# DLRM tower with a two-layer CIN: tails of two groups in one masked operand, P's tiles 0 and 1 split, P ahead of A on TensorE, 128-row spreads

## The reference, cut to what matters

```python
e = stack([tbl_f[ids[:, f]] for f in range(32)], axis=1)      # 512 x 32 x 64
z  = einsum('bhd,bfd->bhfd', e, e)                            # layer 1: 32 x 32 products
y  = relu(einsum('bcd,oc->bod', z.reshape(B, 1024, D), w0) + b0)
hidden, direct1 = y[:, :64], y[:, 64:]
z  = einsum('bhd,bfd->bhfd', hidden, e)                       # layer 2: 64 x 32 products
direct2 = relu(einsum('bcd,oc->bod', z.reshape(B, 2048, D), w1) + b1)
z  = concatenate([direct1, direct2], axis=1).sum(-1)          # 512 x 192
h  = relu(concatenate([z, dense_ctx], 1) @ W_top1 + b_top1)
h  = relu(h @ W_top2 + b_top2);   return h @ W_top3
```

## Time and profile before

| what | value |
|---|---|
| runs | 1076.74, 1075.27, 1078.74 us (median 1076.74) |
| the profiled execution | 1077.73 us, of which the span is 1075.9 us |
| mean granted TensorE clock | 0.995 of full |
| TensorE busy | 1028.1 us (96%) |
| VectorE busy | 932.3 us (87%) |
| GpSimd busy | 916.9 us (85%) |
| ScalarE busy | 724.9 us (67%) |
| DMA | 183.87 MB, 171 GB/s on average |

### The profile page before, as it was taken

One profiled execution on the slowest core, in us unless ns is written; L12 is line 12 of the kernel. 1 busy time (PEld: TensorE's weight loads), 2 busy tenths in 40 slices (PEclk: granted clock), 3 DMA queues, 4 the chain that ended last, 5 costly groups with the idle time before them and its releaser, 6 DMA issues.

```text
span 1075.9 us, 10627 instructions
## 1 busy us (share of the span) xinstructions
PE 1028.1 (96%) x3447; PEld 649.9 (60%) x3447; DVE 932.3 (87%) x609; ACT 724.9 (67%) x794; POOL 916.9 (85%) x299
## 2 busy tenths in 40 slices
PE   2199999999999999999999999999999999999999
PEld 1035566666666666666666666666666666666664
DVE  2069999999998999999999899999989888988881
ACT  5036666677777677777776677677777777777761
POOL 6507877989999999999999999999998988898880
PEclk9989999999999999999999999999999999999999
DMA  6467877878788778777887787788776777677730
GB/s 170 103 148 189 192 184 179 192 188 189 177 191 191 171 183 191 185 188 173 195 188 172 170 193 179 175 195 190 181 172 162 177 176 171 162 177 181 159 76 0
DMA packets 140633, 183.87 MB, mean 171 GB/s; under 512 B 55633, under 2 KB 56273, under 8 KB 140450
## 3 DMA queue, kind: packets, MB, share of 16 engines
q1 hardware_dynamic: 135970, 178.93, 70.5%
q0 software_dynamic: 4096, 4.20, 2.2%
q10 hardware_dynamic: 512, 0.07, 0.0%
HBM read 174.66 MB, written 8.39 MB: 170 GB/s over the span
## 4 chain that ended last, share of the span: by engine, by line
PE 75%; DVE 8%; DMA 6%; issue 4%; SPq 4%; POOL 3%; ACT 1%; ACTq 0%; DVEq 0%
PE py L633 34%; PE py L649 12%; PE py L639 12%; PE py L640 12%; DVE zf L544 5%; DMA xs<-x_dram 5%; POOL emb L333 3%; SPq L274 1%; SPq L268 1%; SPq L285 1%; PE py L654 1%; DVE zl L564 1%; DVE pzS L553 1%; DVE zS L557 0%; PE py L668 0%
## 5 line engine op out<-in xcount | busy, mean ns | idle before, releaser
L343 POOL TENSOR_TENSOR zl<-zf,zh 128x2048 fp32r<-128x2048 f32 x167 | 767.7, 4610 | 98.8 <-ACT zh L416 96.8
L544 DVE TENSOR_TENSOR zf<-xs,hid 128x2048 f32<-128x2048 f32 x256 | 583.0, 2283 | 53.3 <-ACT hid L431 49.4
L633 PE MATMUL py<-zf,wf 128*128 128x512 f32 x1080 | 488.3, 595 | 1.9 <-DVE zf L544 1.9
L416 ACT ACTIVATE zh<-zf 128x2048 fp32r<-128x2048 f32 x185 | 353.5, 1911 | 98.9 <-DVE zf L544 95.7
L633 PEld LDWEIGHTS py<-zf,wf 128*128 128x128 f32 x1080 | 205.0, 190 | 212.7 <-issue 197.4
L639 PE MATMUL py<-zh,wh 128*128 128x512 f32 x740 | 290.1, 392 | 1.3 <-ACT zh L416 1.3
L640 PE MATMUL py<-zh,wl 128*128 128x512 f32 x740 | 289.8, 392 | 0.0
L649 PE MATMUL py<-zl,wh 128*128 128x512 f32 x740 | 228.0, 430 | 0.0
L649 PEld LDWEIGHTS py<-zl,wh 128*128 128x128 f32 x740 | 139.4, 188 | 69.4 <-issue 46.4
L333 POOL DMA_INDIRECT emb<-in_tbl,idx x128 | 149.0, 1164 | 30.5 <-issue 25.5
L639 PEld LDWEIGHTS py<-zh,wh 128*128 128x128 f32 x740 | 139.0, 188 | 34.6 <-ACT zh L416 3.0
(11 more groups left out here) (77 smaller groups left out, 338.5 us busy)
## 6 DMA issues: line engine op xcount, KB each, us to landing
xs<-x_dram SPq DMA_DIRECT2D x512, 256.0 KB, 5.3
xs<-x_dram SPq DMA_DIRECT2D x504, 64.0 KB, 2.1
x_dram<-emb SPq DMA_DIRECT2D x68, 64.0 KB, 5.6
emb<-in_tbl,idx POOLq DMA_INDIRECT x128, 4.7
x_dram<-emb SPq DMA_DIRECT2D x20, 96.0 KB, 5.4
x_dram<-emb SPq DMA_DIRECT2D x4, 384.0 KB
xs<-in_L_rec_w SPq DMA_DIRECT2D x2, 512.0 KB, 4.6
xs<-in_L_rec_w SPq DMA_DIRECT2D x1, 1024.0 KB, 7.3
```

The lines of the kernel that those rows point to most:

```text
L343: pool.tensor_tensor(zl[:, q], zf[:, s], zh[:, q].bitcast(F32), ALU.subtract).then_inc(lo["P"], 1)
L416: act.activation(zh[:, q], zf[:, s], ACT.Copy).then_inc(hi, 1)
L544: dve.tensor_tensor(zf[:, slot(u)], left, right, ALU.mult).then_inc(mult, 1)
L633: mm = pe.matmul(y, wf[:, w, h], zf[:, s, h], start=first and h == 0, stop=ends and h == T - 1)
```

## The change

**Tails of two groups.** Groups 2q-1 and 2q form pair q (group 0 is its own; PAIRS = 33). The operands of the tail product are two SBUF tensors `x0_pair` and `xt_pair`, of which rows 0 to 63 are the odd group's and rows 64 to 127 the even one's; each is loaded by four DMAs, one of the two tensors in each period. One VectorE product per pair makes `pzS`, ScalarE copies its high part to `zS_high`, and one scalar_tensor_tensor computes `zS` = `pzS` x `low_rows` - `zS_high`, where `low_rows` is 0 or 1 per block of 32 rows. The weights `wS` carry the signs. The tail matmul of a group takes 64 rows of `zS` and `wS`.

**Direct sums of two groups.** ScalarE writes the direct channels of two neighbouring groups into the two halves of `dir1` in SBUF, and VectorE sums both in one instruction into `sums1`. ScalarE places the sums into `zd` after every 16 groups (eight small copies in all).

**P's tiles 0 and 1 split.** A new mode H holds for P(g), g >= 2, if C(g-1) is not in mode V: 46 units. Tiles 2 and 3 stay fp32 (four passes), tiles 0 and 1 are split: ScalarE makes `zhP`, VectorE makes `zlP` after C's product, and TensorE does six fp32r passes. The last of them raises `y1_ready`. C of group 0 goes from mode V to mode P.

**Order on TensorE.** From period 1 on: main P(g+1) (tiles 2 and 3, or all), late B(g-1), the high half of P, tail(g+1), main A(g), the low half of P, late A(g), and then as before.

**The start.** `x32` and `spreads` have 128 rows; the rows from 32 on are set to zero by VectorE. The batches of the first gathers are 12, 12, 5 and 3 tables (before 12, 12, 6 and 2), and the load of field 31 into `x32` is issued by SP.

```diff
+    if name == "P" and g >= 2 and mode(("C", g - 1)) != "V":
+        return "H"
     if name in "PD" or unit == ("A", 0):
         return "F"
...
-        return "P" if g % 2 else "V"
+        return "P" if g % 2 or g == 0 else "V"
...
-FIRST_BATCHES = [(0, 0, 12), (0, 12, 12), (0, 24, 6), (0, 30, 2)]
+FIRST_BATCHES = [(0, 0, 12), (0, 12, 12), (0, 24, 5), (0, 29, 3)]
...
+def pair_groups(q):
+    if q == 0:
+        return 0, 0
+    return 2 * q - 1, min(2 * q, LAST)
+
+def pair_of(g):
+    return (g + 1) // 2, 0 if g % 2 or g == 0 else 1
...
-        x32 = sb("x32", [F, N])
+        x32 = sb("x32", [P, N])
...
-        spreads = sb("spreads", [F, T + 2, P])
+        spreads = sb("spreads", [P, T + 2, P])
...
# SP
+                if n == 3:
+                    sp.wait_ge(x32_cleared, 2)
+                    load_x32(sp, 31, x32_last)
...
-            def load_xt(k):
-                if k >= 2:
-                    sp.wait_ge(s_mult, k)
+            def load_pair(q, buf, r):
+                k = pair_groups(q)
+                if k[1] % GC == 0:
+                    sp.wait_ge(x_stored[k[1] // GC], 16 * STORES[k[1] // GC])
+                sp.wait_ge(s_mult, q)
                 for j in range(4):
-                    sp.dma_start(xt[F * j:F * j + F], run_of_rows(k, 16)).then_inc(xt_in, 16)
+                    sp.dma_start(buf[F * j:F * j + F, :], run_of_rows(k[j // 2], r)).then_inc(pair_in, 16)
...
                 if g + 2 < G:
-                    load_xt(g + 2)
+                    load_pair(g // 2 + 2, xt_pair if g % 2 else x0_pair, 16 if g % 2 else 0)
...
# ScalarE
             def copy_x0(k):
                 act.wait_ge(x0_in, 64 * k)
-                act.wait_ge(s_mult, k)
+                if k >= 2:
+                    act.wait_ge(mult, NTH["P", k - 1])
...
+                if mode(u) == "H":
+                    act.wait_ge(mult, NTH[u])
+                    if NTH_HALF[u] > 1:
+                        act.wait_ge(y1_ready, HALVES[NTH_HALF[u] - 2][1] + 1)
+                    act.activation(zhP[:], zf[:, slot(u), 0:2], ACT.Copy).then_inc(hi_half, 1)
...
-            def high_s(k):
-                act.wait_ge(s_mult, k + 1)
-                if k >= 1:
-                    act.wait_ge(y1_ready, k)
-                act.activation(zS[:], pzS[:], ACT.Copy).then_inc(s_hi, 1)
+            def high_s(q):
+                act.wait_ge(s_mult, q + 1)
+                if q >= 1:
+                    act.wait_ge(s_lo, q)
+                act.activation(zS_high[:], pzS[:], ACT.Copy).then_inc(s_hi, 1)
...
             def finish_dir1(k):
-                act.activation(py1[H:P, k % 2], py1[H:P, k % 2], ACT.Relu, bias=bias0[H:P]).then_inc(dir1_ready, 1)
+                if k >= 2:
+                    act.wait_ge(sum1_done, k // 2)
+                half = slice(H * (k % 2), H * (k % 2) + H)
+                act.activation(dir1[half, :], py1[H:P, k % 2], ACT.Relu, bias=bias0[H:P]).then_inc(dir1_ready, 1)
...
# VectorE
-                left, right = (xt, px0[:]) if k >= 1 else (xt_first, x0_first[:])
+                left, right = (xt_pair[:], x0_pair[:]) if q >= 1 else (xt_first, x0_first[:])
                 dve.tensor_tensor(pzS[:], left, right, ALU.mult).then_inc(s_mult, 1)
 
-            def low_s(k):
-                dve.wait_ge(s_hi, k + 1)
-                dve.tensor_tensor(zS[H:P], pzS[H:P], zS[H:P].bitcast(F32), ALU.subtract).then_inc(s_lo, 1)
+            def low_s(q):
+                dve.wait_ge(s_hi, q + 1)
+                if q >= 1:
+                    dve.wait_ge(y1_ready, 2 * q - 1)
+                dve.scalar_tensor_tensor(zS[:], pzS[:], low_rows[:], zS_high[:].bitcast(F32), ALU.mult, ALU.subtract).then_inc(s_lo, 1)
 
             def low(u):
+                if mode(u) == "H":
+                    dve.wait_ge(hi_half, NTH_HALF[u])
+                    dve.tensor_tensor(zlP[:], zf[:, slot(u), 0:2], zhP[:].bitcast(F32), ALU.subtract).then_inc(lo_half, 1)
...
-            def sum_1(k):
-                dve.wait_ge(dir1_ready, k + 1)
-                dve.tensor_reduce(zd[H:P, NS * k:NS * k + NS], py1[H:P, k % 2].rearrange("p (b d) -> p b d", d=D),
+            def sum_1(j):
+                dve.wait_ge(dir1_ready, 2 * j + 2)
+                dve.tensor_reduce(sums1[:, NS * j:NS * j + NS], dir1[:].rearrange("p (b d) -> p b d", d=D),
                                   AX_X, ALU.add).then_inc(sum1_done, 1)
...
                 products(("A", g))
-                sum_1(g)
+                if g % 2:
+                    sum_1(g // 2)
                 if g + 1 < G:
                     products(("P", g + 1))
-                    products_s(g + 1)
+                    if g % 2 == 0:
+                        products_s(g // 2 + 1)
                 products(("C", g))
                 if g + 1 < G:
-                    low_s(g + 1)
+                    low(("P", g + 1))
+                    if g % 2 == 0:
+                        low_s(g // 2 + 1)
...
# TensorE
+            def main_half(u):
+                if mode(u) == "H":
+                    pe.wait_ge(hi_half, NTH_HALF[u])
+                    for h in range(2):
+                        pe.matmul(bank(u), whP[:, h], zhP[:, h], start=False, stop=False)
+                        pe.matmul(bank(u), wlP[:, h], zhP[:, h], start=False, stop=False)
+
+            def late_half(u):
+                if mode(u) == "H":
+                    pe.wait_ge(lo_half, NTH_HALF[u])
+                    pe.matmul(bank(u), whP[:, 0], zlP[:, 0], start=False, stop=False)
+                    mm = pe.matmul(bank(u), whP[:, 1], zlP[:, 1], start=False, stop=True)
+                    mm.then_inc(y1_ready, 1)
+
             def tail(k):
-                pe.wait_ge(s_lo, k + 1)
-                pe.matmul(py1[:, k % 2], wS[:], zS[:], start=False, stop=True).then_inc(y1_ready, 1)
+                q, half = pair_of(k)
+                rows = slice(H * half, H * half + H)
+                pe.wait_ge(s_lo, q + 1)
+                ends = mode(("P", k)) == "F"
+                mm = pe.matmul(py1[:, k % 2], wS[rows, :], zS[rows, :], start=False, stop=ends)
+                if ends:
+                    mm.then_inc(y1_ready, 1)
...
             for g in range(G):
-                main(("A", g))
+                if g == 0:
+                    main(("A", g))
+                if g + 1 < G:
+                    main(("P", g + 1))
                 if g >= 1:
                     late(("B", g - 1))
                 if g + 1 < G:
-                    main(("P", g + 1))
+                    main_half(("P", g + 1))
                     tail(g + 1)
+                if g >= 1:
+                    main(("A", g))
+                if g + 1 < G:
+                    late_half(("P", g + 1))
                 late(("A", g))
```

More of the change, by code:

```diff
@@ L78 @@
 UNITS = [u for g in range(-1, G) for u in period(g)]
-WHOLE = [u for u in UNITS if mode(u) == "F"]
-SPLIT = [u for u in UNITS if mode(u) != "F"]
+WHOLE = [u for u in UNITS if mode(u) in "FH"]
+SPLIT = [u for u in UNITS if mode(u) in "PV"]
+HALVES = [u for u in UNITS if mode(u) == "H"]
 LOW = {m: [u for u in SPLIT if mode(u) == m] for m in "PV"}
@@ L84 @@
 NTH_SPLIT = {u: i + 1 for i, u in enumerate(SPLIT)}
+NTH_HALF = {u: i + 1 for i, u in enumerate(HALVES)}
 NTH_LOW = {u: i + 1 for m in "PV" for i, u in enumerate(LOW[m])}
@@ L131, in dlrm_tower @@
         bias1 = sb("bias1", [P, 1])
-        xs = sb("xs", [P, 3 * T + 2, N])
+        xs = sb("xs", [P, 3 * T + 1, N])
+        x0_pair = sb("x0_pair", [P, N])
+        xt_pair = sb("xt_pair", [P, N])
         zf = sb("zf", [P, ZF, T, N])
@@ L212, in need_used @@
         def need_used(eng, u):
-            if mode(u) == "F":
+            if mode(u) in "FH":
                 eng.wait_ge(used_whole, NTH_WHOLE[u])
@@ L216, in need_used, with load_x32 @@
                 eng.wait_ge(used_split, NTH_SPLIT[u])
+        def load_x32(eng, f, landed):
+            eng.dma_start(x32[f:f + 1, :], emb[0:NS, 0, f, :]).then_inc(landed, 16)
         block = ctx.enter_context(nc.Block())
@@ L300, in _ @@
             load_xd(1)
-            load_xt(1)
+            load_pair(1, x0_pair, 0)
+            load_pair(1, xt_pair, 16)
             load_xe(0)
@@ L364, in _ @@
             act.wait_ge(turns_ready, 1)
+            act.wait_ge(x32_cleared, 2)
             for n, (first, step) in enumerate([(0, 0)] + [(4 * t, 1) for t in range(T)] + [(16, 0)]):
-                act.activation(spreads[:, n].rearrange("p (j i) -> p j i", i=F), view(turns, first, [[step, 4], [1, F]], F),
+                act.activation(spreads[0:F, n].rearrange("p (j i) -> p j i", i=F), view(turns, first, [[step, 4], [1, F]], F),
                                ACT.Copy).then_inc(turns_ready, 1)
@@ L446, in finish_2 @@
                 act.activation(py2[:, g % 2], py2[:, g % 2], ACT.Relu, bias=bias1[:]).then_inc(dir2_ready, 1)
-            for n in range(len(FIRST_BATCHES)):
-                load_x32(n)
+            for n in range(2):
+                _, f, m = FIRST_BATCHES[n]
```

(20 more changed lines are left out.)

101 lines of the change are left out of this document (65 added, 36 removed).

## The result

| | before | changed |
|---|---|---|
| median of 6 runs each, us | 1076.12 (1074.8 to 1080.0) | 1193.45 (1191.34 to 1195.54) |
| span of the profiled execution, us | 1075.9 | 1191.3 |
| end of tail 0 on TensorE | 66.7 | 59.6 |
| tail 1 to tail 11 | 158.7 | 161.0 |
| tail 11 to tail 43 | 492.2 | 590.9 |

The ratio is 1.1081, 95% interval 1.1057 to 1.1105: 117 us slower, where +49 was forecast. The table cuts each execution at the ends of tail matmuls. 99 us of the loss lie in the 32 middle periods.

The account below looks back on a forecast made before the run. TensorE was taken to bound the kernel, without gaps, at about 15.36 us a period. Start -6, early +2, middle +33 and late +20 sum to +49 on 1077.73: 1126 us, own range 1096 to 1150, full range 1077 to 1154.

Parts of the forecast that it names:

- TensorE's own terms: TensorE's passes: split P -0.34 us per unit (-15.6 in all), 64-row tails +0.4 each (+26 in all).
- The 64-row tail: Tail matmul among 128-row ones: each change of row count costs 0.2 us, two per tail, 26 us over 64 tails.
- The start: Earlier spreads by about 1.3 us and a clock that stays full with 128 rows: together -6 us (bounds -1.3, -7).
- Early periods: Periods 1 to 10: TensorE needs 31.9 us a pair, +0.5 a pair, +2 us with the ramp.
- The exclusion: A VectorE operation with two SBUF operands and a GpSimd subtraction exclude each other for their whole length.
- Late periods: Periods 43 to 62: VectorE waits for GpSimd, +1.0 us a period, +20 us over 20 periods (10 to 31).
- The tie at low A: Late even periods, tail product level with GpSimd's low A: 16.6 us if VectorE is first, 18.7 if GpSimd is.
- The middle: Periods 11 to 42: 14 us of VectorE waits in six periods, +1.04 a period, +33 us over 32 (16 to 51).
- the tail product's wait: Periods 11 to 42, tail product held by GpSimd: waits of 2.0, 0.2 and 1.9 us in six periods.
- P ahead of A: TensorE's new order: asks for P's product about 2.7 us earlier, 2 us in hand, so it costs nothing.
- Tails only: Rival: the exclusion falls into gaps and TensorE stays the bound, +4.4 us, 1081 us; chance 0.07.
- The gain comes through: Rival: TensorE bounds and 64 rows cost nothing, -6 - 15.6, 1055 us; chance 0.14.

Follow-up runs that it names:

- e8: The kernel before, with the tail product reading x0 from an SBUF copy made by ScalarE in place of PSUM: 1279.54 us, ratio 1.187.
- e1: The changed kernel, with the tail product reading one operand from PSUM (ScalarE copies x0_pair there): 1127.95 us, ratio 1.047.
- e15: The changed kernel with its 4-byte tensor low_rows padded to 64 bytes, nothing else: 1195.26 us, ratio 1.108.
- e18: The changed kernel, padded to 64 bytes and with TensorE's order of before: 1168.50 us, ratio 1.085.
- e9: The changed kernel, not padded, with GpSimd's second gather moved from ahead of low B to behind it: 1158.50 us, ratio 1.075.
- e16: The changed kernel, padded, with TensorE's order of before and GpSimd's second gather moved behind low B: 1120.69 us, ratio 1.039.
- e12: e11 with TensorE's order of before in place of P ahead of A: 1064.50 us, ratio 0.987.
- e3: The changed kernel with the tail product reading one operand from PSUM and P whole in fp32: 1103.51 us, ratio 1.025.
- e11: e3 with 128-row tails and low_rows padded to 64 bytes: 1070.96 us, ratio 0.993.
- e14: e6 with one unused tensor of 4 bytes per partition ahead of the operands, no instruction changed: 1079.08 us, ratio 1.001.
- e6: The kernel before with the new start alone (128-row x32 and spreads, new first batches, one load on SP): 1070.87 us, ratio 0.994.

## Why the forecast had the sign and missed the size

**TensorE's own terms held.** The 64-row tail was put at 0.4 us and measured 0.39. The start was put at -6 and gave -7.1 (59.6 against 66.7), at full clock. Early periods were put at 31.9 a pair; they took 32.04, and 31.79 with the padding.

**The exclusion held.** The half lows and tail products end a fixed 1.08 and 0.57 us after a GpSimd subtraction. e8 shows the exclusion alone, e1 its removal from the tail products. The sum of its waits is another matter (the middle, below).

**Late periods held, the number by luck.** +18.5 was measured, +20 forecast. The forecast averaged two cases of a tie, +0.5 and +1.55 a period. The tie at low A fell to VectorE each time, the cheaper case, for which +0.5 is 10 us; with TensorE's 15.42 for the odd periods in place of 15.2 it would be 13. For that case 16.6 and 15.42 were given, and 16.87 and 15.55 came: +0.85 a period. The 0.13 of difference in the second is the placement (15.38 in e15); that in the first is not explained.

**The middle failed: +33 forecast, +98.7 measured.** VectorE's time between tails 11 and 43 can be added up from the traces. A wait is a duration less 0.69 (tail product) or 1.21 (half low); the forecast's column is its 4.1 and 9.75 us in six periods, over 32.

| us | forecast | changed | e18 order of before | e9 gather moved | e16 both |
|---|---|---|---|---|---|
| waits in tail products | 22 | 84.5 | 84.8 | 22.3 | 22.2 |
| waits in half lows | 52 | 18.5 | 21.3 | 34.6 | 38.1 |
| VectorE idle | 0 | 39.8 | 16.2 | 45.5 | 12.4 |
| the middle | 525 | 590.9 | 568.6 | 554.5 | 522.6 |

The rest, VectorE's own work, is 446 to 452 us in each column (the forecast's 84.4 in six periods are 450). So the tail products' waits and the idle time were put too low, by 62 and 40 us, and the half lows' waits too high, by 33, which hid a third of the miss. Two steps are at fault.

The first is the tail product's wait, put at 2.0, 0.2 and 1.9 us in six periods. It was measured at 5.7, 5.7 and 4.3. The bookkeeping ended each wait at the end of the subtraction then running, though it had GpSimd's low B run on into the next period with low A right behind it. A tail product that waits does not get in between these two (a half low does between low A and low C, as shown above). Held so long, VectorE comes to its half lows when low A is over: that is why these waited less than forecast, and why they wait more again once the gather is moved. What the earlier trace rows shows held the hint: GpSimd's 9.15 for two subtractions without a gap at 440.88, and line 564 at 449.50 waiting for the end of the last. It met only the second, so the row didn't decide. Price: 35 us (e9), 48 once the order is right (e18 to e16).

The second is "P ahead of A: 2 us in hand, so nothing". The step asked only whether P's product is there in time. It left out what is moved back: B's last passes of the group before, behind P's main ones. ScalarE's ReLU waits for them and VectorE's second sum for it: 14.0 us of idle VectorE in the window shown, at the time when VectorE bounds. With the order of before VectorE's idle time in the middle falls from 37.3 (e15) to 16.2 us (e18), and the middle from 588.4 to 568.6. Price: 27 us (e18), 38 with the gather moved (e9 to e16, which has the padding too), 6.5 in a kernel that TensorE bounds (e12).

With both taken out, e16 is the kernel that the forecast described: 1120.7 us against 1126, middle 522.6 against 525, early 158.7 against 161, late 322.9 against 327. So the remaining terms are right together, in part because two errors offset each other: the table has 14 us less in the half lows than forecast and 12 us of idle time that was not in the forecast. The range ended at 1154 because its upper ends varied the waits' length and never their number.

**The rivals.** Nearest to "Tails only" is e3, which has neither the waits nor the split: 1103.5, where the forecast's terms for it, -6 and +26, give 1096; the other 8 us are the placement. "The gain comes through" was never near: with all of e11's edits the time is 1071, and there P's split was tried in the early groups alone, where it gives 2 us. What the change gains is the start; what was free of cost besides it is 128-row tails and the pairing.

**Open.** The changed kernel's clock in the middle is below full:

```profile
240.00:815.00 575.00, 514.74 (x1691) 332.29 (x1691) 536.72 (x265) 364.13 (x382) 461.15 (x146) 0.94 0.65 154
```

A clock of 0.94 in the mean over 575 us is some 70 us at half (the 1.2 GHz level), in stretches that follow TensorE's gaps. In e16, where the gaps are small, 20 us of the middle are at half. That the clock is a large part of the loss is unlikely: of the changed kernel's six executions four have a mean clock of 0.956 to 0.958 and spans of 1191.3 to 1193.7, two have 0.973 and 1189.5 and 1189.8. These two spend some 36 us less at half and are only 2 to 4 us faster. A run that holds the clock there would settle it.

Open too is what lets a waiting VectorE operation in between two subtractions of GpSimd: whether the second is ready by the time it starts to wait, its size, its output, or its place.

## What to carry to other kernels

Before a VectorE operand moves from PSUM to SBUF, look at what GpSimd does in that moment, and reckon with every subtraction up to its next gap, not only with the one running: here the tail products waited for all of them, the half lows for one. When work is moved ahead on a queue, the price is in what it is moved past: follow that to the engine that bounds. And pad small tensors, or put them last: four bytes ahead of the operands cost as much as a real edit.

## What of the hardware was unexpected

- A VectorE operation with two SBUF operands can wait over two back-to-back GpSimd subtractions: 6.40 us for one of 0.69, 11 of 33 tail products in the changed kernel, 21 of 64 in e8. Ten half lows of the changed kernel got in between two. The Trainium skill, SBUF — State Buffer, section SBUF: two separate sides, gives the pair to whichever starts first, for the whole instruction; the runs agree, and add that the one that waits is not always next.
- Operands 4 bytes further on in SBUF: an fp32r pass every 0.233 us in place of 0.229, some 8 us in e14. The weights did not move in e14; which of the others it is was not tried. fp32 passes kept 0.59 us of length.
- A 64-row matmul among 128-row ones: 0.39 us, 0.2 for each change.
- TensorE's clock stays full through spreads of 128 rows with zeros (1.00 in e6), where it fell to half at 55.4 us with 32 rows; e6 also starts its spreads earlier.
